# Decoder of two layers on one core: the mixture's products in another order, its weight split in two, and the layer norms' scaling on ScalarE

## What is computed

```python
x = _layernorm(x + _L0_attn_ref(x, ...))
x = _layernorm(x + _L0_xattn_ref(x, ctx_2048, mask_BxS2_bk0))
x = _layernorm(x + _L0_ffn_ref(x, ...))
x = _layernorm(x + _L1_attn_ref(x, ...))
x = _layernorm(x + _L1_xattn_ref(x, ctx_2048, ctx_2048))
x = _layernorm(x + _L1_ffn_ref(x, ...))
def _layernorm(x, axis=-1, eps=1e-05):
    return (x - mean) / sqrt(var + eps)
```

## Time and profile before

| | |
|---|---|
| median of 3 runs | 2201.52 us (2200.05 to 2203.65) |
| the profiled execution | 2202.97 us, its span 2200.7 us |
| PE busy | 1942.1 us, 88% of the span |
| DVE busy | 1418.7 us, 64% |
| ACT busy | 1062.4 us, 48% |
| POOL busy | 644.2 us, 29% |
| granted PE clock, mean | 0.938 |

### The profile page before, as it was taken

How to read it: one execution, slowest core, us unless ns; L and a number is a source line. 1 busy time by engine, 2 the same in 40 slices (tenths; PEclk the granted TensorE clock), 3 DMA queues, 4 the chain that set the end, 5 groups by cost and what they waited for, 6 DMA issues and landing times. The chain is left out here.

```text
span 2200.7 us, 36115 instructions
## 1 busy us (share of the span) xinstructions
PE 1942.1 (88%) x12856; PEld 1192.5 (54%) x12856; DVE 1418.7 (64%) x2641; ACT 1062.4 (48%) x2121; POOL 644.2 (29%) x552
## 2 busy tenths in 40 slices
PE   7888876989999999978999999996688886899998
PEld 4555553457777777753545445453355553355553
DVE  5666575466777677766847567587699956554334
ACT  4666634224333333323726456372699983344332
POOL 3655500022334233300101101012676760222320
PEclk8999987989999999998999999998599967999999
DMA  4000003111111011004110010002800003577533
GB/s 141 25 25 1 1 1 120 63 40 34 48 48 48 25 48 48 24 2 139 39 39 20 20 39 18 0 1 44 208 3 2 3 2 134 172 177 189 124 71 91
DMA packets 95263, 125.39 MB, mean 57 GB/s; under 512 B 8440, under 2 KB 51704, under 8 KB 95120
## 3 DMA queue, kind: packets, MB, share of 16 engines
q1 hardware_dynamic: 88400, 107.71, 16.0%
q0 software_dynamic: 6720, 15.73, 3.9%
HBM read 101.60 MB, written 18.61 MB: 55 GB/s over the span
## 5 line engine op out<-in xcount | busy, mean ns | idle before, releaser
L1142 POOL TENSOR_TENSOR wl<-stage,wh 128x512 fp32r<-128x512 f32 x80 | 117.8, 1504 | 393.2 <-DVE wh L1137 393.2
L1586 POOL TENSOR_TENSOR Zl<-z,Zh 128x512 f16<-128x512 f32 x32 | 51.1, 1597 | 492.8 <-ACT Zh L1747 492.8
L77 PE MATMUL PS<-XTh,wh 128*128 128x512 f16 x416 | 160.4, 386 | 19.8 <-ACT t L2170 19.0
L2646 POOL TENSOR_TENSOR PTl<-P,PTh 128x512 f16<-128x512 f32 (+2 forms) x160 | 149.9, 946 | 65.2 <-ACT PTh L2801 62.5
L79 PE MATMUL PS<-XTh,wl 128*128 128x512 f16 x416 | 160.2, 385 | 0.0
L78 PE MATMUL PS<-XTl,wh 128*128 128x512 f16 x416 | 160.1, 385 | 0.0
L1357 ACT ACTIVATE h<-PS,bup 128x512 f32<-128x512 f32 x64 | 44.1, 689 | 235.7 <-PE PS L79 235.7
L2800 ACT ACTIVATE P<-PS 128x512 f32<-128x512 f32 (+3 forms) x256 | 144.0, 562 | 15.8 <-PE PS L2737 15.3
L2801 ACT ACTIVATE PTh<-PS 128x512 f16<-128x512 f32 (+3 forms) x256 | 145.5, 568 | 0.0
L2815 DVE TENSOR_REDUCE M<-PS 128x1 f32<-128x640 f32 (+3 forms) x128 | 127.0, 1011 | 4.1 <-PE PS L2719 4.1
L2737 PE MATMUL PS<-QS,KS 98*128 98x512 f16 (+3 forms) x256 | 99.4, 389 | 27.0 <-ACT PTh L2801 15.1
(11 more groups left out here) (382 smaller groups left out, 6014.0 us busy)
## 6 DMA issues: line engine op xcount, KB each, us to landing
stage<-in_ffn_W SPq DMA_DIRECT2D x18, 1024.0 KB, 5.2
stage<-in_ffn_Wg SPq DMA_DIRECT2D x9, 1024.0 KB, 5.3
stage<-in_ffn_Wup SPq DMA_DIRECT2D x16, 512.0 KB, 3.8
stage<-in_ffn_Wdn SPq DMA_DIRECT2D x16, 512.0 KB, 3.6
wq<-in_attn_wq SPq DMA_DIRECT2D x4, 1024.0 KB, 6.0
C<-in_ctx SPq DMA_DIRECT2D x8, 512.0 KB, 8.8
stage<-in_ffn_Wsw SPq DMA_DIRECT2D x16, 256.0 KB, 3.4
stage<-in_attn_WV SPq DMA_DIRECT2D x16, 256.0 KB, 3.8
```

Of the source, the lines that this page charges most:

```text
L77: pe.matmul(out, a[0], b[0], start=start, stop=False, skip_group_check=True)
L1142: self.c.nc.gpsimd.tensor_tensor(self.piece(self.low[q], ch), self.piece(self.stage, ch), plain(self.piece(self.high[q], ch)), ALU.subtrac ...
L2646: ops.tensor_tensor(PTl[:, (CT * n + kt) % RING, cols], P32[:, (CT * n + kt) % SLOTS, cols], PTh[:, (CT * n + kt) % RING, cols], ALU.subtr ...
```

## The change

Four edits. In the mixture, `down(n)` is cut in two halves of four tiles, and `up(n+1)` for m = 2, 3 goes between them; on DVE the adds are cut likewise, `h_part` for m = 2, 3 goes between the halves, three of the five casts go ahead of the adds and two (of Wdn) behind. In all six norms the scaling moves from DVE to ACT as one `Identity` activation with scale `rstd` and bias `shift` = -mean * rstd; DVE computes `shift` (128x1) instead, and epsilon becomes the bias of the square root, so `veps` goes. The cross-attentions call `root` and `normalize` in alternation on ACT. The casts of the first expert move in `phase_cross0` to the end of the loop's pass t = 5.

```diff
     def moments(self, dve, t):
...
-        dve.wait_ge(self.mv_done, t + 1)
-        nc.vector.tensor_scalar(self.veps[:, t:t + 1], self.mv[:, t, 1:2], EPS, None, ALU.add).then_inc(self.veps_done, 1)
 
     def root(self, act, t):
-        act.wait_ge(self.veps_done, t + 1)
-        self.c.nc.scalar.activation(self.std[:, t:t + 1], self.veps[:, t:t + 1], ACT.Sqrt).then_inc(self.std_done, 1)
-
-    def normalize(self, dve, t):
+        act.wait_ge(self.mv_done, t + 1)
+        self.c.nc.scalar.activation(self.std[:, t:t + 1], self.mv[:, t, 1:2], ACT.Sqrt,
+                                    bias=self.c.eps[:]).then_inc(self.std_done, 1)
+
+    def factors(self, dve, t):
         nc = self.c.nc
         dve.wait_ge(self.std_done, t + 1)
         nc.vector.reciprocal(self.rstd[:, t:t + 1], self.std[:, t:t + 1]).then_inc(self.rstd_done, 1)
         dve.wait_ge(self.rstd_done, t + 1)
-        nc.vector.tensor_scalar(self.X[:, t, :], self.X[:, t, :], self.mv[:, t, 0:1], self.rstd[:, t:t + 1],
-                                ALU.subtract, ALU.mult).then_inc(self.normed, 1)
+        nc.vector.scalar_tensor_tensor(out=self.shift[:, t:t + 1], in0=self.mv[:, t, 0:1], scalar=-1.0,
+                                       in1=self.rstd[:, t:t + 1], op0=ALU.mult, op1=ALU.mult).then_inc(self.shift_done, 1)
+
+    def normalize(self, act, t):
+        act.wait_ge(self.shift_done, t + 1)
+        self.c.nc.scalar.activation(self.X[:, t, :], self.X[:, t, :], ACT.Identity, bias=self.shift[:, t:t + 1],
+                                    scale=self.rstd[:, t:t + 1]).then_inc(self.normed, 1)
...
     def act_step(self, act, t):
         if self.norm and t < NT:
             self.root(act, t)
+        if self.norm and 1 <= t <= NT:
+            self.normalize(act, t - 1)
...
             def body(n, q):
                 second(n, q)
                 up(n + 1, 1 - q, (0, 1))
-                down(n, q)
+                down(n, q, 0)
                 up(n + 1, 1 - q, (2, 3))
+                down(n, q, 1)
...
-                for t in range(NT):
-                    add(n, e, t, dst)
                 if more:
-                    weights.split_hi(dve, n + 2, q)
-                for m in (2, 3):
-                    h_part(n + 1, m)
+                    weights.split_hi(dve, n + 2, q, (0, 1))
+                for b in range(B):
+                    for t in range(b * QT, (b + 1) * QT):
+                        add(n, e, t, dst)
+                    if b == 0:
+                        for m in (2, 3):
+                            h_part(n + 1, m)
+                if more:
+                    weights.split_hi(dve, n + 2, q, (2,))
...
@@ phase_cross0, ACT (phase_cross1 the same)
+            for t in range(NT + 1):
+                if t < NT:
+                    norm.root(act, t)
+                if t > 0:
+                    norm.normalize(act, t - 1)
             for t in range(NT):
-                norm.root(act, t)
...
@@ phase_cross0, DVE
+                if t == 5:
+                    weights.split_hi(dve, 0, 0)
             for t in range(NT - 1):
-                norm.normalize(dve, t)
-            weights.split_hi(dve, 0, 0)
+                norm.factors(dve, t)
             output(NT - 1)
             norm.moments(dve, NT - 1)
-            norm.normalize(dve, NT - 1)
+            norm.factors(dve, NT - 1)
```

More of the change, by code:

```diff
@@ L98, in __init__ @@
         self.identb = self.sb(ctx, "identb", [P, P], BF16)
+        self.eps = self.sb(ctx, "eps", [P, 1], F32)
         self.PS = ctx.enter_context(nc.psum_tensor("PS", [P, 8, 512], F32))
@@ L158, in __init__ @@
         self.mv = c.sb(ctx, "mv", [P, NT, 2], F32)
-        self.veps = c.sb(ctx, "veps", [P, NT], F32)
+        self.shift = c.sb(ctx, "shift", [P, NT], F32)
         self.std = c.sb(ctx, "std", [P, NT], F32)
@@ L163, in __init__ @@
         self.mv_done = c.sem(ctx, "mv_done")
-        self.veps_done = c.sem(ctx, "veps_done")
+        self.shift_done = c.sem(ctx, "shift_done")
         self.std_done = c.sem(ctx, "std_done")
@@ L224, in dve_step @@
         if self.norm and 1 <= t <= NT:
-            self.normalize(dve, t - 1)
+            self.factors(dve, t - 1)
         if not self.to_dram and 3 <= t < NT + 3:
@@ L282, in _ @@
         def _(dve):
+            nc.vector.memset(c.eps[:], EPS)
             dve.wait_ge(ident_in, 16)
@@ L1005, in _ @@
                 shared_g(1, m)
-            for t in range(NT):
-                norm.root(act, t)
+            for t in range(NT + 1):
+                norm.act_step(act, t)
         @block.vector
@@ L1084, in _ @@
                 if t > 0:
-                    norm.normalize(dve, t - 1)
+                    norm.factors(dve, t - 1)
             for q in range(QT):
@@ L1088, in _ @@
                 norm.moments(dve, QT + q)
-                norm.normalize(dve, QT + q - 1)
-            norm.normalize(dve, NT - 1)
+                norm.factors(dve, QT + q - 1)
+            norm.factors(dve, NT - 1)
 class ExpertWeights:
@@ L1131, in load, with split_hi @@
             sp.dma_start(self.stage[i][:], src).then_inc(self.w_in[i], 16)
-    def split_hi(self, dve, n, q):
+    def split_hi(self, dve, n, q, some=None):
         for ch, (i, h) in enumerate(self.PARTS):
+            if some is not None and i not in some:
+                continue
             if h == 0:
@@ L1286, in second, with down @@
                         turn_w(n // NE)
-            def down(n, q):
+            def down(n, q, b=None):
                 final = isinstance(n, int) and n % NE == NE - 1
-                pe.wait_ge(w_lo, CH * n + LAST[2])
-                if isinstance(n, int) and n % NE == 0:
+                if b != 1:
+                    pe.wait_ge(w_lo, CH * n + LAST[2])
+                if isinstance(n, int) and n % NE == 0 and b == 0:
                     pe.wait_ge(gate.shifted, n // NE + 1)
@@ L1297, in down @@
                     pe.wait_ge(silu_done, UP * (n + 1))
-                for t in range(NT):
+                for t in range(NT) if b is None else range(b * QT, (b + 1) * QT):
                     if t % QT == 0:
@@ L2479, in _ @@
                     context_high(u)
+            for t in range(NT + 1):
+                if t < NT:
+                    norm.root(act, t)
+                if t > 0:
+                    norm.normalize(act, t - 1)
             for t in range(NT):
-                norm.root(act, t)
-            if not norm.to_dram:
-                for t in range(NT):
-                    norm.high(act, t)
+                norm.high(act, t)
         @block.vector
@@ L2545, in _ @@
                     context_low(u)
+                if t == 5:
+                    weights.split_hi(dve, 0, 0)
             for t in range(NT - 1):
-                norm.normalize(dve, t)
-            weights.split_hi(dve, 0, 0)
+                norm.factors(dve, t)
             output(NT - 1)
             norm.moments(dve, NT - 1)
-            norm.normalize(dve, NT - 1)
-            if not norm.to_dram:
-                for t in range(NT):
-                    norm.low(dve, t)
+            norm.factors(dve, NT - 1)
+            for t in range(NT):
+                norm.low(dve, t)
 def phase_cross1(c, **end):
```

## The result

| | before | changed |
|---|---|---|
| median of 4 runs | 2200.78 us | 2175.15 us (2171.70 to 2177.81) |
| ratio | 1 | 0.9883, 95% interval 0.9862 to 0.9903 |
| the profiled execution | 2202.97 us, span 2200.7 | 2176.73 us, span 2175.0 |
| PE busy | 1942.1 us | 1936.2 us |
| DVE busy | 1418.7 us | 1346.3 us |

The changed kernel is 25.6 us (1.2%) faster; 30.9 were forecast, and the time of 2175.15 lies within the range. Against the kernel before, as a whole, the stages of the first layer's mixture give 18.5 of the 25.7 us by which the span fell, its cross-attention 5.5, the last phase 2.8. A stage runs here from the last low part of one phase to that of the next.

What follows compares the result with a forecast made beforehand. PE was taken as the limit (88% busy), with one wait per expert coming from DVE's order. Terms of -16.7, -1.0, -4.0, -3.1, -2.6, -1.2, -2.3 and 0 sum to -30.9, forecasting 2170.6 us, range 2162 to 2187.

Steps and rivals of the forecast that it cites:

- Twelve bubbles: Mixture: PE's wait for `Hl` in `second`, behind five DVE casts, goes in 12 bodies at 1.4 us each: -16.7 us.
- the cover: Mixture: slack before PE waits, 6 us for the second `Hl` pair and 5 us for the first add.
- The feared stretch of the three casts: Mixture, DVE: casts beside POOL's work might stretch by 2.6 times and end 4.8 us later, just inside the adds' cover.
- second and third rival: Second: the bubble moves, 16.7 us don't come, 2187.3, chance 0.12. Third: `down`'s second half waits for adds, 2213, chance 0.03.
- Six of them fit ahead of the last output: End of cross0: six of the eight scalings on ACT fit ahead of `output(7)`; part of the -4.0 us term.
- The last one adds 0.72 - 0.55 to the chain: End of cross0: the last scaling takes 0.72 us on ACT, 0.55 on DVE, and `high(0)` waits for it.
- n = 7, -1.0: Round's end: PE waits 2.45 us before `down`; an earlier second `Hl` brings part, between 0 and 2.45, taken as -1.0.
- Four tails: Norms' scaling moved to ACT: mixture's end -3.1, attn1 -2.6, cross1 -1.2, last phase -2.3 us; together 9.2.
- lie in its holes, if they aren't on the chain: All norms: ACT is at 48% over the span, so 48 new scalings (35 us) lie in its idle time.
- the first rival: Ends of phases: ACT takes over the tails, 9.2 us are lost and attn0 pays 2.5: 2182.3 us, chance 0.15.

Runs made afterwards that it cites:

- the extra pass: The changed kernel with one more ACT pass, a copy of the tile onto itself, ahead of each scaling in the norms: 2198.90 us.
- the fourth experiment: The kernel before with `Hl` of m = 2, 3 ahead of the five casts on DVE, PE's order kept: 2208.06 us, ratio 1.0029.

## Why the prediction was right, and where it was off

**Right: the mixture's order.** Twelve bubbles of 1.4 were forecast, -16.7 (12 x 1.4 is 16.8), with bodies of 27.7. From the first `second` of a round to that of its last expert the time fell from 204.44 to 196.22 and from 203.76 to 195.81 us, 16.2 in all. The two marks of the cover were where the prediction put them: `Hl` ready 24.4 us into the body (24.1 forecast), the first add 15.6 into it (16 to 17). The feared stretch of the three casts didn't come: 0.73 us each, not up to 2.6. The second and third rival have their mechanism in the run with DVE's half of the reorder: there the wait moved to `down`, and it is the adds that PE waits for. With PE's half alone the old wait on `Hl` grew from 1.2 to 6.5 us. With both halves neither came.

**Right in size, mixed in cause: cross0.** The forecast of -4.0 had the casts at some 4.8 and the longer chain of the last tile. The tail fell by 3.3. Alone, the casts brought 4.9 to the last output, as forecast. Two steps failed. "Six of them fit ahead of the last output": six scalings do stand there, but they hold it up. On ACT root and scaling follow each other every 0.89 us, DVE's factors wait for each root, and the last output is queued behind them on DVE; that costs 0.7 us. "The last one adds 0.72 - 0.55 to the chain": ACT's order puts the scaling of the seventh tile behind the root of the eighth, so two scalings stand between that root and the first high part, 1.50 us (464.42 above). Putting this scaling back on DVE gave 2.5 us back in all.

**Wrong: n = 7, -1.0.** From `second` to `down` it took 9.54 us before and 9.50 now. The bubble in that `second` is gone, and PE's wait before `down` grew by as much as it had been. On DVE g of m = 1 takes 1.42 us now, behind the casts of Wdn that the change put there:

```profile
688.52 0.75 DVE L1147 CAST wh<-stage 128x512 fp32r<-128x512 f32 x2
...
691.26 1.42 DVE L1455 TENSOR_TENSOR g<-h,s 128x512 f32<-128x512 f32 x1 [0.28 <-ACT s L1393]
```

Ahead of the last expert of the second round, n = 15, no casts stand, since there is no expert left to split. There the same g takes 0.69, and PE waits 2.14 us before `down`, not 2.87:

```profile
933.01 0.69 DVE L1455 TENSOR_TENSOR g<-h,s 128x512 f32<-128x512 f32 x1 [0.70 <-ACT s L1393]
```

So the casts of Wdn, with POOL's splitting behind them, cost about as much here as the earlier `Hl` gave; no run leaves out these casts alone.

**Mis-sized: the norms.** Four tails were to give 9.2 us. They gave 1.9 at the mixture's end (3.1 forecast), 2.05 in attn1 (2.6), 0.4 in cross1 (1.2) and 2.1 in the last phase (2.3, though only 0.45 in four other profiles of the same code); attn0 lost 0.3, cross0 some 2.5. The sum is 3 to 4 in the first profile, about 2 with the smaller figure of the last phase, and 2.6 by the medians when done alone. At the mixture's end pairs of profiles with the clock alike give 2.2 and 2.5 (25.17 against 22.94, 25.75 against 23.28). Two terms failed. The scaling costs 0.81 us, not the 0.72 that I chose between 0.63 and 0.80; and the root with its epsilon as bias costs 0.29, which I hadn't counted as a change at all (0.20 in the profile of before, at 1817.66). The larger one is the sentence that ACT's scalings "lie in its holes, if they aren't on the chain", which left open whether they are: DVE was freed, but another engine's time per tile came next. In attn1 a step was 2.99 us (adds at 1516.92 and 1519.91) and is 3.02 now, since DVE waits for PE's products; only the lag was won (timeline of DVE):

```profile
1489.59 0.69 DVE L1847 SCALAR_TENSOR_TENSOR X<-PS,X 128x512 f32<-128x512 f32 x1 [0.55 <-PE PS L79]
...
1492.61 0.69 DVE L1847 SCALAR_TENSOR_TENSOR X<-PS,X 128x512 f32<-128x512 f32 x1 [0.55 <-PE PS L79]
```

and at the end PE waits for the scaling, 1.94 us (1498.42; before it was 1.45 and 2.35 for `XTl`):

```profile
1498.42 0.65 PE L211 MATMUL PS<-ident,X 128*128 128x128 f32 x4 [1.94 <-ACT X L197]
```

So the first rival, that ACT takes over the tails, came true in part: in cross0, and in the closing chain elsewhere. Here the price of the Trainium skill was the better one: "ScalarE: Activation LUTs", section *What ACT_TABLE_LOAD costs*, gave 0.80 us as an estimate, and the trace has 809 ns; its 93 ns for a pointer operand also fits the root's 0.29 against 0.20. Its rule that additions and multiplications belong on VectorE, for which it gives a factor of up to about 3 in bf16 (here, in float32, it is 0.55 us on DVE against 0.81 on ACT), holds here for cross0, where the scalings stand in a row on ACT, and not for the mixture's end and attn1, where DVE was the limit.

**Not forecast: the clock.** The stage of the second cross-attention took 2.2 us more in the profile after, though its tail fell by 0.4; no edit touches what lies ahead of the tail. Windows of the stretch that differs, changed and before (same place in the phase):

```profile
1721.00:1741.00 20.00, 17.11 (x253) 11.10 (x252) 18.54 (x28) 16.26 (x39) 11.68 (x14) 0.79 0.01 2
```
```profile
1746.00:1766.00 20.00, 17.68 (x292) 11.96 (x289) 19.35 (x33) 18.81 (x46) 14.70 (x17) 0.97 0.01 3
```

The granted clock is 0.79 in place of 0.97 with the same work ahead of it. In the other profiles this stage takes between 0.4 and 7.1 us more than in the one before; the longest has the extra pass in its tail. What makes the clock fall in one execution and not in another stays open. The first cross-attention shows the other sign: its stage fell by 5.5 us, its tail by 3.3. The other 2.2 lie ahead of its first output, 53.76 us before and 51.52 now for the same 176 matmuls, at a granted clock of 0.73 and 0.77; the run with the casts alone, whose code there is that of before, takes 51.6 at 0.77 too.

The clock also explains the two values of the last phase. Windows of the changed kernel's two profiles at the same place, 3.48 us behind the last g:

```profile
2159.04:2162.46 3.42, 3.42 (x18) 1.53 (x17) 3.19 (x13) 3.17 (x6) 0.00 (x0) 1.00 0.26 98
```
```profile
2159.52:2162.94 3.42, 3.42 (x10) 1.22 (x9) 3.06 (x12) 3.16 (x6) 0.00 (x0) 0.50 0.26 98
```

In the second the granted clock is 0.50, the lower of its two levels (1.2 GHz, not 2.4), PE makes 10 matmuls where it made 18, and the tail is 21.08 us in place of 19.41. All four profiles with 21.1 have such a stretch there, and the changed norms' profiles with 19.4 have none. With the norms on DVE it costs nothing: the order alone has it, the kernel before hasn't, and both take 21.54, since DVE sets the pace there. So moving the norms gave 2.1 us where the clock held and 0.45 where it didn't, because PE's pace now shows.

That the whole came so near the forecast is partly luck: rounds and tails of the first profile give 25.6 us, the span fell by 25.7, and what the clock gave ahead of the first cross-attention's tail (2.2) it took in the second (2.6).

## What to carry to other kernels

A wait that returns in every body is worth more than all ends of phases together, but the order that removes it must be changed on both engines: one half alone brought nothing, the other cost 85 us. When work moves to an engine that is idle on average, look at each place for what stands behind it in that engine's queue: scalings in a row on ACT at the end of cross0 took back 2.5 of the 6 us that the same scaling gave elsewhere. And what stands on DVE beside POOL's splitting should be something that it doesn't slow (here the adds, which read PSUM) or that nobody waits for.

## What the runs showed that I had not expected

Five casts in a row took 5.05 us, and three and two apart from each other 2.94 in sum; DVE's busy time in one body fell from 20.45 to 16.45 us by its order (16.58 with the order alone). Two instructions of 0.69 us each took 3.48 us together beside POOL's splitting, `Hl` in the kernel before and g in the fourth experiment, while adds that read PSUM kept their 0.73 to 0.75. Bodies with a wait of 6.5 us had a granted clock of 0.86 to 0.91 in place of 1.00, and PE was busy 2.8 us longer in the one shown. One stretch at a granted clock of 0.50 cost 1.7 us in the last phase once DVE had been relieved there, and nothing before. Two pointer operands on ACT are not free: 0.81 us for the scaling against 0.63 for an activation of the same size without any, also from SBUF.
